# A graph network kernel: last additions, layer norm and router of layer 0 in one stage

## The reference, cut to what matters

```python
xn = _layernorm(x, axis=-1)
x = x + _L0_gnn_ref(xn, edge_index, ...) + _L0_mix_ref(xn[None], ...)[0]
x = x + _L0_ffn_ref(_layernorm(x, axis=-1)[None], L0_ffn_router_w, ...)[0]
...
# _L0_ffn_ref, per token (here: per node); 8 experts, the best 2 are used
logits = tokens @ router_w.T
probs = softmax(logits); rw, re = top_k(probs, 2); rw = rw / rw.sum(-1)
out = tokens + sum over experts of combine[:, e] * (gelu(tokens @ w1[e] + b1[e]) @ w2[e] + b2[e])
```

## Time and profile before

| | us |
|---|---|
| median of 3 runs | 1409.33 |
| lowest and highest | 1406.69, 1414.96 |
| the profiled execution | 1415.98 |
| its span (first to last instruction) | 1414.0 |

### The profile page before, as it was taken

One profiled execution on the slowest core, in us unless ns is written; L12 is line 12 of the kernel. 1 busy time (PEld: TensorE's weight loads), 2 busy tenths in 40 slices (PEclk: granted clock), 3 DMA queues, 4 the chain that ended last, 5 costly groups with the idle time before them and its releaser, 6 DMA issues. The chain is left out here.

```text
span 1414.0 us, 22751 instructions
## 1 busy us (share of the span) xinstructions
PE 1169.0 (83%) x7588; PEld 921.5 (65%) x7588; DVE 754.9 (53%) x2376; ACT 454.0 (32%) x916; POOL 595.6 (42%) x698
## 2 busy tenths in 40 slices
PE   3777789876972899617999999999999869966997
PEld 2677779443641677416878888888888645535886
DVE  5999981276578344384545555454356431252332
ACT  2477770331321332111324333333333233221110
POOL 3366640003121677402776676766667000003442
PEclk9899999997965899959999999999999989987999
DMA  5000000410025233365666666656565056576551
GB/s 126 1 2 2 2 2 2 107 12 1 0 71 192 78 98 99 92 161 156 199 175 191 183 198 181 188 180 190 176 192 180 6 171 186 117 159 206 172 177 53
DMA packets 97276, 165.62 MB, mean 117 GB/s; under 512 B 15506, under 2 KB 59182, under 8 KB 96774
## 3 DMA queue, kind: packets, MB, share of 16 engines
q1 hardware_dynamic: 71669, 90.69, 22.5%
q0 software_dynamic: 25488, 73.39, 17.9%
HBM read 138.40 MB, written 27.63 MB: 117 GB/s over the span
## 5 line engine op out<-in xcount | busy, mean ns | idle before, releaser
L2266 POOL DMA_INDIRECT em_gathered<-edge_table,el_which x313 | 301.7, 964 | 132.1 <-issue 74.2
L2278 PE MATMUL em_projected<-em_w,em_attr 128*128 128x256 f32 x1252 | 283.1, 384 | 7.6 <-PEq L1897 7.6
L2278 PEld LDWEIGHTS em_projected<-em_w,em_attr 128*128 128x128 f32 x1252 | 240.4, 193 | 42.5 <-issue 9.9
L2356 DVE TENSOR_TENSOR em_hidden<-em_projected,em_gathered 128x512 f32<-128x512 f32 (+1 forms) x157 | 108.3, 690 | 205.2 <-PE em_projected L2278 127.3
L2378 ACT ACTIVATE em_hidden<-em_hidden 128x512 f32<-128x512 f32 (+1 forms) x157 | 98.7, 628 | 271.5 <-DVE em_hidden L2356 271.4
L434 POOL TENSOR_SCALAR nm_hot_a<-nm_order,ek_places 128x125 bf16<-128x125 int16 x150 | 99.7, 673 | 51.1 <-PE nm_banks L558 47.7
L446 DVE TENSOR_SCALAR nm_hot_key<-nm_key_order,ek_keys 128x100 bf16<-128x100 int16 x500 | 118.4, 263 | 0.0
L2689 POOL DMA_INDIRECT oe_hidden<-oe_table,oo_node x27 | 25.9, 959 | 179.4 <-DMA oe_table<-state 130.0
L2761 PE MATMUL oe_banks<-oe_wd,xn_T 128*128 x432 | 98.1, 381 | 0.0
L445 DVE TENSOR_SCALAR nm_hot_a<-nm_order,ek_places 128x125 bf16<-128x125 int16 x350 | 94.6, 272 | 0.0
L2761 PEld LDWEIGHTS oe_banks<-oe_wd,xn_T 128*128 128x128 f32 x432 | 80.7, 192 | 9.8
(11 more groups left out here) (482 smaller groups left out, 2267.0 us busy)
## 6 DMA issues: line engine op xcount, KB each, us to landing
em_attr<-in_edge_attr_sets SPq DMA_DIRECT2D x156, 256.0 KB, 3.6
oe_table<-state SPq DMA_DIRECT2D x20, 448.0 KB
oe_wd<-in_ffn_Wd SPq DMA_DIRECT2D x8, 1024.0 KB
em_gathered<-edge_table,el_which POOLq DMA_INDIRECT x313, 3.6
mx_w<-in_ffn_w SPq DMA_DIRECT2D x16, 256.0 KB
oe_table<-state SPq DMA_DIRECT2D x1, 2248.8 KB
state<-in_x SPq DMA_DIRECT2D x5, 448.0 KB
state<-in_x SPq DMA_DIRECT2D x1, 2240.0 KB
```

The lines of the kernel that those rows point to most:

```text
L2266: nc.gpsimd.indirect_dma_start(out=gathered[:, n % GATHERED, :], out_offset=None, in_=table, in_offset=bass.IndirectOffsetOnAxis(ap=lanes. ...
L2278: last = nc.tensor.matmul(projected[:, k % BANKS, n % 2, :], attr[:, k % ATTR_RING, (n % 2 * KB + f) * 128:(n % 2 * KB + f + 1) * 128], w1 ...
L2356: nc.vector.tensor_tensor(pair_slots(k), projected[:, k % BANKS, 0:width, :], gathered[:, at:at + width, :], ALU.add).then_inc(pre_ready, 1)
```

## The change

`sage_and_mix` becomes `sage_to_gate`. It takes in the layer norm and the router, and `layer_norm` "ln1" goes.

- The 20 tiles are two halves of ten (`FIRST`). As soon as the first ten are joined and measured, VectorE makes their mean and variance, joins two more, inverts the root and makes a shift. ScalarE then normalises these ten tiles itself (scale and shift by row), while VectorE joins the other ten. After those, VectorE makes the second half's mean and root and normalises these tiles.
- TensorE's list now has, tile by tile, the two transposes of a normalised tile (`turn_rows`), the two back transposes of a later tile (`turn_back`) and two router matmuls of the tile before (`route`). `route` has the tile's 125 nodes as the fixed side and the router's 8 columns as the moving one, so the logits come out with nodes on partitions and need no transposing.
- ScalarE copies each transposed tile to `xn_T` (`keep`), two slots instead of four.
- The router's weights are loaded in the stage before, with the other weights; their place has 8 columns in each block and isn't cleared.
- `mixture` loses its router steps. The gate's steps come first in VectorE's list and `origin.vector_first` second. Inside the gate the cast of `order` comes after the subtraction of the peak. In the other layer the gate keeps its bias and its way, with the cast moved likewise.

The core of the diff:

```diff
+                def turn_rows(t):
+                    if t < FIRST:
+                        pe.wait_ge(first_normed, t + 1)
+                    else:
+                        pe.wait_ge(last_normed, t - FIRST + 1)
+                    if t >= 2:
+                        pe.wait_ge(row_kept, t - 1)
+                    for k in range(KB):
+                        last = nc.tensor.transpose(turned[:, t % 2, k * P:(k + 1) * P], xn[:, t, k * 128:(k + 1) * 128], c.ident[:P, :P])
+                    last.then_inc(row_turned, 1)
+
+                def route(t):
+                    pe.wait_ge(row_kept, t + 1)
+                    for k in range(KB):
+                        last = nc.tensor.matmul(logits[:, t, :], xn_T[:, k, t * P:(t + 1) * P], weights.router[:, k, :],
+                                                start=(k == 0), stop=(k == KB - 1))
+                    last.then_inc(logits_ready, 1)
...
+                pe.wait_ge(own_kept, PIECES)
+                pe.wait_ge(h_ready, PIECES)
+                for t in range(FIRST + 4):
+                    turn_back(t)
+                for t in range(TILES):
+                    turn_rows(t)
+                    if t + FIRST + 4 < TILES:
+                        turn_back(t + FIRST + 4)
+                    if t >= 1:
+                        route(t - 1)
+                route(TILES - 1)
...
+                root(0)
+                act.wait_ge(row_scaled, 1)
+                for t in range(FIRST):
+                    nc.scalar.activation(xn[:, t, 0:DIM], x[:, t, :], ACT.Identity, bias=row_shift[:, t:t + 1],
+                                         scale=row_std[:, 0, t:t + 1]).then_inc(first_normed, 1)
+                    if t >= 2:
+                        keep(t - 2)
+                for t in range(FIRST - 2, FIRST):
+                    keep(t)
+                root(1)
+                for t in range(FIRST, TILES):
+                    keep(t)
...
+                for t in range(FIRST):
+                    join(t)
+                measure_row(FIRST - 1)
+                find_row_var(0)
+                join(FIRST)
+                join(FIRST + 1)
+                find_row_std(0)
+                nc.vector.scalar_tensor_tensor(row_shift[:], row_mean[:, 0], -1.0, row_std[:, 0], ALU.mult, ALU.mult).then_inc(row_scaled, 1)
+                for t in range(FIRST + 2, TILES):
+                    join(t)
                 measure_row(TILES - 1)
+                find_row_var(1)
+                find_row_std(1)
+                for t in range(FIRST, TILES):
+                    i = t - FIRST
+                    nc.vector.tensor_scalar(xn[:, t, 0:DIM], x[:, t, :], row_mean[:, 1, i:i + 1], row_std[:, 1, i:i + 1],
+                                            ALU.subtract, ALU.mult).then_inc(last_normed, 1)
+                dve.wait_ge(logits_ready, TILES)
+                nc.vector.tensor_copy(raw[:], logits)
...
-                nc.vector.memset(router[:], 0.0).then_inc(cleared, 1)
+                gate.vector_steps(dve)
                 origin.vector_first(dve)
-                gate.vector_steps(dve, logits, logits_ready, CHUNKS)
                 way.vector_steps(dve, gate)
```

More of the change, by code:

```diff
@@ L1157, in piece, with turn_back @@
                     last.then_inc(turn_ready, 1)
[L1159 to L1164, removed]
+                def turn_back(t):
                     if t % 4 == 0:
@@ L1187, in _, with root, keep @@
                     nc.scalar.activation(piece, piece, ACT.Relu, bias=shift[:, d:d + 1], scale=std[:, d:d + 1]).then_inc(rectified, 1)
+                def root(g):
+                    act.wait_ge(row_var_ready, g + 1)
+                    nc.scalar.activation(row_std[:, g], row_var[:, g], ACT.Sqrt).then_inc(row_std_ready, 1)
+                def keep(t):
+                    act.wait_ge(row_turned, t + 1)
+                    nc.scalar.activation(xn_T[:, :, t * P:(t + 1) * P],
+                                         turned[:, t % 2, 0:KB * P].rearrange("p (k n) -> p k n", k=KB), ACT.Copy).then_inc(row_kept, 1)
+                root(0)
[10 more added lines that the diff above has]
+                    keep(t)
             @block.vector
@@ L1409, in then @@
             chain.wait(dve)
[L1411 to L1416, removed]
+        if logits is not None:
+            dve.wait_ge(ready, count)
             then(nc.vector.tensor_tensor(self.raw[:], logits, across(self.bias), ALU.add))
@@ L1419, in vector_steps @@
         nc.vector.tensor_tensor(self.raw[:], self.raw[:], over(self.peak), ALU.subtract).then_inc(self.shifted, 1)
+        dve.wait_ge(self.numbered, 1)
+        then(nc.vector.tensor_copy(self.order[:], self.order_i[:]))
         dve.wait_ge(self.exped, 1)
@@ L1625, in tensor_steps, with mixture @@
         last.then_inc(self.found, 1)
-def mixture(p, c, A, state, x, xn, xn_T, first_w, first_b):
+def mixture(p, c, A, state, x, xn, xn_T, first_w, first_b, raw):
     nc = p.nc
@@ L1760, in bring_down @@
                     last.then_inc(down_ready, 1)
-                pe.wait_ge(router_loaded, 16)
-                for first, last_chunk in ((0, 4), (4, CHUNKS)):
-                    for k in range(KB):
-                        for q in range(first, last_chunk):
-                            lane = q % 4 * LANE
-                            last = nc.tensor.matmul(banks[lane:lane + LANE, 4 + q % 4, 0:CHUNK] if q < 4 else banks[0:LANE, 3, 0:CHUNK],
-                                                    router[:, k, :], xn_T[:, k, q * CHUNK:(q + 1) * CHUNK], start=(k == 0), stop=(k == KB - 1))
-                            if k == KB - 1:
-                                last.then_inc(routed, 1)
-                for q in range(CHUNKS):
-                    pe.wait_ge(logits_kept, q + 1)
-                    for t in range(q * 4, (q + 1) * 4):
-                        last = nc.tensor.transpose(logits[:, t, :], logits_T[:, t * P:(t + 1) * P], c.ident[:EXPERTS, :EXPERTS])
-                    last.then_inc(logits_ready, 1)
                 way.tensor_steps(pe, gate)
```

74 lines of the change are left out of this document (47 added, 27 removed).

## The result

The changed kernel took 1417.52 us (median of seven executions, 1414.44 to 1419.42); the kernel before took 1409.33 beside it (seven, 1403.11 to 1414.96). The ratio is 1.0045, 95% interval 1.0027 to 1.0064: 6.3 us slower, 3.8 to 9.0 (the plain medians are 8.2 us apart). The forecast was 1411.5, 2.2 us slower. The change went to the side it gave, and 1.0045 is inside its bound of 0.5%, though the interval reaches past that bound. By the ratio the time is 1415.7 us, inside the range of 1400 to 1417; the plain median lies just above it. The sum came out near by luck: the stage ended 10.6 us later than its term said, and the gate and what follows gave back 8.1 us more than its term said.

A forecast was written before the change was run, and what follows sets the result against it. The prediction took VectorE's joins, then GpSimd's additions, to bound the touched stretch; a stage 3.05 us longer less 0.8 us in the mixture gave 2.2 us more, 1409.3 to 1411.5 us, range 1400 to 1417.

The forecast's parts named there:

- What binds: Before the change: VectorE paces the joins; GpSimd's additions to 429.11 us, not the router, end the gate's first step.
- The join of tile 14 waits for TensorE: Fused stage, second half of joins: fixed TensorE order makes a join wait for a ScalarE normalisation; no separate size.
- TensorE's six instructions a tile: Fused stage: two row transposes, two back transposes, two router matmuls; 0.71 us a tile at 2.4 GHz, 1.3 at 1.2.
- The clock rises near 403: Fused stage: with TensorE's rise to 2.4 GHz, mixture 3.05 us later; at 1.2 GHz to the end, about 9.5.
- ScalarE's normalisation: Fused stage: ScalarE normalises a tile in 0.44 us, with its copy 0.71 us a tile.
- The second root behind keep(9): Fused stage, second statistics: ScalarE's root queues behind two copies and runs at 408.3, so VectorE waits 0.35 us.
- L1423 waits for GpSimd's last addition: Mixture's gate: the product of prob and total ends at 15.3 us, signal to TensorE 19.8 us after the mixture's start.
- rival 1: Mixture's gate: each two-input instruction waits for one addition only; signal at 11.2 us, total 1404.5 us; chance 0.30.
- Another 1.5 us lost afterwards: After the gate's signal, under one-addition waits: GpSimd runs to 17 us, costing another 1.5 us.
- Four casts before the signal: Gate: casts formerly in VectorE's idle time now stand before the signal to TensorE, adding 0.55 us.
- What stays: Dispatch, origins and gather onward unchanged, 1 us allowed both ways; expert weights down 17 us before TensorE wants them.
- rival 3: Fused stage: TensorE's clock stays at 1.2 GHz, stage ends near 423.5; 8.7 us more, 1418 us; chance 0.12.

The follow-up runs named there:

- e12: The kernel before, unchanged, executed once more to look at its subtraction behind the logits copy; 1414.47 us in its one execution.
- e2: Changed kernel with one fp32 router matmul per tile instead of two (half of the features, outputs not the reference's); 1412.43 us, 0.9989 of the kernel before.
- e5: Kernel before with the router's weights loaded two stages early and eight columns read without padding; 1492.62 us on a slower chip, 0.9952 of the kernel before.
- e6: Changed kernel's split norm with the old router put back in the mixture and its weights loaded early; 1498.88 us on a slower chip, 0.9987 of the kernel before.
- e8: Changed kernel with eight of GpSimd's additions moved ahead of its index patterns; 1505.74 us on a slower chip, 1.0038 of the kernel before.
- e11: Kernel before with the router's weights loaded early and no padding, a repeat of e5 on another chip; 1406.45 us, 0.9948 of the kernel before.
- e4: Changed kernel with router load, matmuls, copies and transposes back in the mixture and casts ahead of the gate, split norm kept; 1414.69 us, 1.0009 of the kernel before.
- e3: Changed kernel with GpSimd's twenty additions x + xn moved from the mixture into the fused stage; 1414.97 us, 1.0012 of the kernel before.
- e1: Changed kernel with filler TensorE matmuls of 512 bf16 columns (32 in all) in the fused stage; 1420.56 us, 1.0046 of the kernel before.

## Why the prediction was right, and where it was not

- **What binds** (VectorE's joins before; GpSimd's additions to 429.11): held. e12 shows the wait of the subtraction again. The prediction made a law of it, though. The join of tile 14 waits for TensorE, as foreseen (0.51 us, at 400.93).
- **TensorE's six instructions a tile** (0.71 us at 2.4 GHz, 1.3 at 1.2): this is the first term that was mis-sized. There were eight passes: at 1.2 GHz two row transposes took 0.45 us (418.03 to 418.48), the four of the router 0.70 (to 419.18), two transposes back 0.43, together 1.58. The sum had 1.3 for that. The last tiles, without the transposes back, took 1.15 us, where 0.56 was taken and "0.85 or more" given for 1.2 GHz. So the missing passes are worth 0.3 us a tile, and the rest of the miss is the clock. The hint stood in the rows: the prediction itself counts "20 matmuls" where the code has ten calls. e2 shows that the missing passes were on the path.
- **The clock rises near 403**: failed. It was 0.50 from 395 to 477 us. With the passes and the root below this gives the mixture's start at +13.7 us (14.5 from the first join) instead of +3.05, beyond even the bound of +9.5. By the prediction's own figures the clock is 6.4 us of the miss (9.5 less 3.05); that leaves 5.0, from the first join, for passes and root.
- **ScalarE's normalisation** (0.44 us): 0.50 from start to start, hidden behind TensorE. **The second root behind keep(9)**: right in kind, wrong in size. It ran at 412.98, and VectorE waited 2.97 us where 0.35 was taken. That was not hidden: TensorE idled 1.24 us behind it, and the tiles lost 1.4. No run moved the root.
- **L1423 waits for GpSimd's last addition**, signal 19.8 us after the start: failed, and this failure is what brought the sum back near the measured time. Now L1521, it took 0.58 us, and the signal came 10.3 us after the start. That is rival 1's reading, which said 11.2. The Trainium skill (SBUF — State Buffer, Who interferes with whom) states that a VectorE instruction with two SBUF inputs contends with a GpSimd instruction that reads SBUF; that the first to issue has the shared ports for its whole instruction it says of VectorE's two-port modes. Carried over to the gate, this agrees with its meetings in the changed kernel and with the subtraction in e5, e6, e8 and e11 (0.50 to 0.91 us), and disagrees with the subtraction in the kernel before (twice) and in e4 (2.27 to 3.44 us).
- **Another 1.5 us lost afterwards** (rival 1): measured. Between count and gather 1.4 us went, in scans that met the last additions: 29.2 us in the changed kernel, 27.8 in e3, where none is left to meet, and 27.9 before.
- **Four casts before the signal** (0.55 us): 2.0 us, since they met additions; 0.5 in e3.
- **What stays**: held. The gather's +4.75 is +5.15 at the last result; the expert weights were not late.
- **The sum.** The outcome is rival 3's stage with rival 1's gate. The text priced them at +8.7 and at 4.8 below the time before, against a forecast of +2.2, but never together. By its own terms the two give 9.5 - 7.9 = 1.6 us, next to the forecast, so that the time alone could not have told them from it. Stage 14.5 longer than before, less 0.8 of an earlier first join, less the 8.9 that gate and count regain, is the 4.75 at the gather.
- **A lever it passed over.** The wait for the router's weights, 4.4 us, was counted among what the additions hide. Removed with the padding that went with it, it gave 7 us, since the long wait went too.

## What to carry to other kernels

Count TensorE's work in the records of the trace, not in the calls of the code: here an fp32 matmul was two weight loads and two passes, so an 8-column matmul took 0.35 us at 1.2 GHz where a transpose of 125 columns took 0.22. An idle wait on TensorE can cost more than its length (4.42 us of waiting for the router's weights made the matmuls behind it 2.7 us longer), so look at the granted clock on both sides of each wait. When two terms of a sum have rivals, price the rivals together too. And before work moves to an engine that seems to wait, look at how long that engine's own instructions are in that loop: GpSimd had nothing free beside its gathers and scatters.

## What the runs showed of the hardware that was not expected

- One and the same kind of meeting had two outcomes. The subtraction waited for one addition in e5, e6, e8 and e11 (0.50 to 0.91 us), and for all that remained in the kernel before, e4 and e12 (2.27, 3.44, 3.08 us). In the three long ones eleven to thirteen additions had run since VectorE last met one (before, a cast met one at 417.48 and the subtraction the next at 427.02; an addition each 0.68 us); in the short ones six at most. But the number of additions still to come parts the same two groups, three to five against nine or more. These are patterns in seven meetings. The cause stays open, and no run varied either alone.
- TensorE's clock fell from 1.00 to 0.50 in e1 at 412.2 us, after 13.20 us with TensorE busy for 10.84 (its last idle time, 1.33 us, ended at 410.67), and did not rise in the 9.60 us after it, busy throughout. In this one execution the clock stayed up 17 us longer than in the changed kernel (412.2 against 395.0), not to the end.
- In the changed kernel GpSimd's additions are stretched, from 0.72 to 0.80 us each, while the gate's products meet them (430.46 to 436.60), and the last two, beside the scans, to 0.97 and 1.03. So such a stretch is longer on both sides. While the casts meet them they stay at 0.72, though the casts wait (0.70 for 0.17).
